# Self-attention rounds of a four-layer Perceiver kernel: statistics one tile further ahead, another order on every engine

## The reference

```python
x = x + L1_attn(layernorm(x))   # 8 heads of 32, keys and values from a latent of 64
x = x + L2_attn(layernorm(x))   # 16 query heads of 8, 4 key heads; RMS norm, rotation
x = x + L3_attn(layernorm(x))   # 16 heads of 8, hyperbolic distance

# L1: probs = softmax(q k^T / sqrt(32));  out = (probs v) Wo
# L2: q, k = rotate(rms_norm(q)), rotate(rms_norm(k))
#     s = 50 tanh(q k^T / sqrt(8) / 50), causal;  out = (softmax(s) v) Wo
# L3: diff = max(|q|^2 + |k|^2 - 2 q k^T, 0)
#     denom = max((1 - |q|^2)(1 - |k|^2), 1e-6)
#     out = (softmax(-arccosh(1 + 2 diff / denom)) v) Wo
```

## Time and profile before

| | |
|---|---|
| median of 3 runs | 7111.27 us (7109.43 to 7120.28) |
| the profiled execution's own time | 7113.01 us |
| its span, first to last instruction | 7110.8 us |
| mean granted TensorE clock | 0.902 of 2.4 GHz |
| busy: TensorE, weight loads, VectorE, ScalarE, GpSimd | 82%, 65%, 55%, 40%, 26% |

### The profile page before, as it was taken

The page is one execution under the profiler, slowest core; times in us unless marked ns, Lnnn a source line. Parts: engine busy times, 40 slices in busy tenths (PEclk is TensorE's granted clock), DMA queues, the critical chain, the costliest instruction groups (busy, mean ns, idle before and its releaser), DMA issues.

```text
span 7110.8 us, 164674 instructions
## 1 busy us (share of the span) xinstructions
PE 5839.7 (82%) x53890; PEld 4596.3 (65%) x53890; DVE 3933.1 (55%) x12136; ACT 2811.1 (40%) x6643; POOL 1823.1 (26%) x2870
## 2 busy tenths in 40 slices
PE   6888888788779998878888998676679987778888
PEld 4666666777447776656665777664457766666666
DVE  5766665444336664544444665664446659964443
ACT  2444443111234442245544555223435542235555
POOL 3444443000013333300000343660014434320000
PEclk9999999999769998999998999678779997779999
DMA  3000000000000000000000110000001100000000
GB/s 126 16 16 16 16 16 8 0 0 0 0 15 30 30 24 0 0 0 0 0 0 9 34 33 24 0 0 0 0 15 33 33 18 0 0 0 0 0 0 12
DMA packets 43764, 93.43 MB, mean 13 GB/s; under 512 B 7696, under 2 KB 28560, under 8 KB 42640
## 3 DMA queue, kind: packets, MB, share of 16 engines
q1 hardware_dynamic: 43664, 92.09, 4.1%
HBM read 88.92 MB, written 3.15 MB: 13 GB/s over the span
## 4 chain that ended last, share of the span: by engine, by line
issue 47%; PE 35%; DVE 8%; POOL 6%; ACT 2%; SPq 1%; POOLq 0%; DVEq 0%; DMA 0%; ACTq 0%
PE psum_banks L548 5%; PE psum_banks L553 4%; PE psum_banks L613 3%; PE psum_banks L657 3%; PE psum_banks L664 2%; PE psum_banks L617 2%; PE psum_banks L1598 2%; PE psum_banks L1574 2%; PE psum_banks L1633 2%; POOL scratch L957 2%; PE psum_banks L1072 1%; DVE scratch L919 1%; POOL scratch L1495 1%; POOL scratch L924 1%; PE psum_banks L1586 1%
## 5 line engine op out<-in xcount | busy, mean ns | idle before, releaser
L2271 PE MATMUL psum_banks<-w_L_ffn_up,x_normed_T 128*128 128x352 f32 (+3 forms) x2112 | 871.8, 535 | 90.4 <-DVE x_normed_T L2413 56.9
L263 POOL TENSOR_TENSOR ln_vareps<-ln_meanvar,ln_eps 128x1 f32<-128x1 f32 x165 | 44.6, 270 | 2794.5 <-DVE ln_meanvar L258 2794.5
L780 DVE TENSOR_REDUCE scratch<-psum_banks 128x2 f32<-128x514 f32 x768 | 531.0, 691 | 411.1 <-PE psum_banks L548 407.0
L699 ACT ACTIVATE scratch<-psum_banks 128x512 f32<-128x512 f32 x768 | 458.5, 597 | 491.1 <-PE psum_banks L558 485.8
L553 PE MATMUL psum_banks<-scratch 32*128 32x128 f32 x6144 | 639.3, 310 | 8.2 <-ACT scratch L699 6.1
L2309 ACT ACTIVATE scratch<-psum_banks 128x176 f32<-128x176 f32 (+3 forms) x1120 | 398.6, 371 | 619.8 <-PE psum_banks L2271 526.9
L548 PE MATMUL psum_banks<-scratch 32*128 32x257 f32 x3072 | 575.5, 441 | 50.2 <-DVE scratch L781 50.1
L2257 PE MATMUL psum_banks<-w_L_ffn_down,scratch 128*128 128x128 f32 x4096 | 563.7, 285 | 10.4 <-ACT scratch L2300 10.4
L2249 PEld LDWEIGHTS psum_banks<-consts,scratch 128*128 128x128 f32 x2144 | 280.5, 154 | 444.7 <-issue 295.5
L2271 PEld LDWEIGHTS psum_banks<-w_L_ffn_up,x_normed_T 128*128 128x128 f32 x2112 | 407.0, 218 | 221.7 <-issue 106.5
L2453 DVE SCALAR_TENSOR_TENSOR scratch<-scratch,psum_banks 128x176 f32<-128x176 f32 (+2 forms) x704 | 257.6, 373 | 524.7 <-ACT scratch L2309 492.2
(11 more groups left out here) (426 smaller groups left out, 14236.7 us busy)
## 6 DMA issues: line engine op xcount, KB each, us to landing
scratch<-in_ctx SPq DMA_DIRECT2D x99, 514.0 KB, 3.5
scratch<-in_ctx_rows SPq DMA_DIRECT2D x130, 128.0 KB, 2.1
w_L_ffn_up<-in_L_ffn_up SPq DMA_DIRECT2D x1, 2992.0 KB, 10.5
w_L_ffn_down<-in_L_ffn_down SPq DMA_DIRECT2D x1, 2112.0 KB, 12.1
w_L_ffn_up<-in_L_ffn_up SPq DMA_DIRECT2D x1, 2080.0 KB, 7.9
x_tokens<-in_x SPq DMA_DIRECT2D x1, 2048.0 KB, 7.7
scratch<-last_values SPq DMA_DIRECT2D x128, 8.0 KB
out<-x_tokens SPq DMA_DIRECT2D x1, 2048.0 KB, 6.3
```

The source lines that it names most:

```text
L699: act.activation(pT[:, b % 2, 2 * h:2 * h + 2].rearrange("p t c q -> p t (c q)"), W, ACT.Exp).then_inc(exp_ready.sem, 1)
L780: dve.tensor_reduce(parts[:, r.t.odd, 2 * h:2 * h + 2, 0, b], S, X_AXIS, ALU.max, negate=True)
L2271: pe.matmul(U[g % 3][:, 0:fw * halves], k.xnT[:, :], up[:, c0:c0 + fw * halves], start=True, stop=True).then_inc(sg["up_written"].sem, 1)
```

## The change

- All three stages: statistics move from tile r+2 to tile r+3 (`third`), to the end of VectorE's round ahead of residual, and `normal` to the end of GpSimd's round. `normalised` stays with tile r+2 and goes to the front of VectorE's round (in the third stage behind two steps). The plan begins one round earlier.
- First stage: on VectorE heads(r-1) goes ahead of operands(r+1).
- Second stage: VectorE's order becomes normalised, rotate, mask, squares, heads, operands, statistics, residual. GpSimd's power is now for tile r+2 and stands behind its two spreads. TensorE's turn(r) goes behind project and middle. ScalarE's take_x goes ahead of Tanh and Exp, take_qkv ahead of take_middle.
- Third stage: TensorE's scores(r+1) go ahead of heads(r-1). 1 - sum is now made on TensorE: the matrix has -1 in place of 1, and a product of a row of ones with itself adds 1 (two products more). take_middle goes, and VectorE reads the result from PSUM. GpSimd does its four spreads in one run.

The diff, cut to its core (`...` for what is left out):

```diff
@@ chain, plan
-    plan = Plan(1, TILES - 3, TILES + 1, 2, -2)
+    plan = Plan(1, TILES - 3, TILES + 1, 2, -3)
@@ GpSimd, one(r)
             if kind == "L1":
-                if r.after:
-                    normal(r.t + 2)
                 if r.coming:
...
                     values(t, s["kv"][:, 256:512])
             if kind == "L2":
-                if r.coming:
-                    pool.wait_ge(ms_ready.sem, ms_ready.at(t, 1))
-                    pool.wait_ge(rotated.sem, rotated.at(r.t, 1))
-                    pool.tensor_tensor(s["r"][:, :], s["ms"][:, :], k.minus_half[:, 0:20], ALU.pow).then_inc(rms_ready.sem, 1)
-                if r.after:
-                    normal(r.t + 2)
...
+                if r.after:
+                    pool.wait_ge(ms_ready.sem, ms_ready.at(r.t + 2, 1))
+                    pool.wait_ge(rotated.sem, rotated.at(t, 1))
+                    pool.tensor_tensor(s["r"][:, :], s["ms"][:, :], k.minus_half[:, 0:20], ALU.pow).then_inc(rms_ready.sem, 1)
...
+            if r.third:
+                normal(r.t + 3)
@@ TensorE
         def middle(t):
-            pe.wait_ge(mid_read.sem, mid_read.at(t + -1, 1))
+            if kind == "L3":
+                pe.wait_ge(operands.sem, operands.at(t + -1, 1))
+            else:
+                pe.wait_ge(mid_read.sem, mid_read.at(t + -1, 1))
...
-                    mm = pe.matmul(MID[:, n * P:(n + 1) * P], k.c("same_head"), s["sq"][:, n * P:(n + 1) * P], start=True,
-                                   stop=True, skip_group_check=True)
+                    cols = slice(n * P, (n + 1) * P)
+                    pe.matmul(MID[:, cols], k.c("minus_same_head"), s["sq"][:, cols], start=True, stop=False,
+                              skip_group_check=True)
+                    mm = pe.matmul(MID[:, cols], one, one, start=False, stop=True, skip_group_check=True)
...
-            if kind != "L3" and r.own:
+            if kind == "L1" and r.own:
                 turn(r.t)
...
+            if kind == "L2" and r.own:
+                turn(r.t)
+            if kind == "L3" and r.coming:
+                scores(r.t + 1)
             if r.turned:
                 heads(r.t + -1)
-            if r.coming:
+            if kind != "L3" and r.coming:
                 scores(r.t + 1)
@@ ScalarE, second stage
-            elif r.own:
+            if kind == "L2" and r.after:
+                take_x(r.t + 2)
+            if kind == "L2" and r.own:
                 act.wait_ge(scores_written.sem, scores_written.at(r.t, 1))
                 act.activation(s["D"], D[:, :], ACT.Tanh, scale=float(1.0 / (CAP * np.sqrt(8.0)))).then_inc(scores_read.sem, 1)
...
@@ VectorE, stats and one_l2(r)
-            if r.after:
-                link(dve.bn_stats(k.stat[:, :], k.X[:, (r.t + 2).index(), :]), r, "stats")
+            if r.third:
+                link(dve.bn_stats(k.stat[:, :], k.X[:, (r.t + 3).index(), :]), r, "stats")
...
-            stats(r)
+            normalised(r)
+            if r.coming:
+                rotate(r)
             if r.own:
...
-            if r.coming:
-                rotate(r)
-            normalised(r)
-            heads(r)
...
                 dve.tensor_scalar(s["ms"], s["ms"], 0.125, 1e-5, ALU.mult, ALU.add).then_inc(ms_ready.sem, 1)
+            heads(r)
...
+            stats(r)
             residual(r)
@@ VectorE, one_l3(r)
-            stats(r)
...
+            normalised(r)
...
-                dve.wait_ge(mid_read.sem, mid_read.at(t, 1))
-                rows_by_head(dve, s["rest"], s["ab"][:, 0:P], k.c("lane_eighth"))
+                dve.wait_ge(mid_written.sem, mid_written.at(t, 1))
+                rows_by_head(dve, s["rest"], MID[:, 0:P], k.c("lane_eighth"))
+                rows_by_head(dve, s["kbd"][:, 2, :], MID[:, P:2 * P], k.c("quad")).then_inc(operands.sem, 1)
...
-            normalised(r)
-            if r.coming:
-                rows_by_head(dve, s["kbd"][:, 2, :], s["ab"][:, P:2 * P], k.c("quad")).then_inc(operands.sem, 1)
             heads(r)
...
+            stats(r)
             residual(r)
```

More of the change, by code:

```diff
@@ L346, in __init__ @@
         r = plan.loop if t.i is not None else t.o
-        self.after, self.coming, self.own, self.turned, self.ended, self.left = (
-            0 <= r + d < TILES for d in (2, 1, 0, -1, -2, -3))
+        self.third, self.after, self.coming, self.own, self.turned, self.ended, self.left = (
+            0 <= r + d < TILES for d in (3, 2, 1, 0, -1, -2, -3))
 class PerTile:
@@ L1191, in one @@
             if r.after:
-                take_x(r.t + 2)
                 if kind == "L1":
-                    take_qkv(r.t + 2)
-            if kind == "L2":
-                if r.coming:
-                    take_middle(r.t + 1)
-                if r.after:
-                    take_qkv(r.t + 2)
+                    take_x(r.t + 2)
+                take_qkv(r.t + 2)
+            if kind == "L2" and r.coming:
+                take_middle(r.t + 1)
             if r.turned:
@@ L1305, in one_l2 @@
                                   ).then_inc(probs_ready.sem, 1)
-            if r.coming:
-                rotate(r)
-            normalised(r)
-            heads(r)
-            if r.coming:
-                t = r.t + 1
-                dve.wait_ge(mid_read.sem, mid_read.at(t, 1))
-                dve.wait_ge(scores_written.sem, scores_written.at(r.t, 1))
-                rows_by_head(dve, s["qbd"][:, 0, :], s["qkT"][:, 0:P], k.c("lane")).then_inc(operands.sem, 1)
             if r.after:
@@ L1321, in one_l2 @@
                 dve.tensor_scalar(s["ms"], s["ms"], 0.125, 1e-5, ALU.mult, ALU.add).then_inc(ms_ready.sem, 1)
+            heads(r)
+            if r.coming:
+                t = r.t + 1
+                dve.wait_ge(mid_read.sem, mid_read.at(t, 1))
+                dve.wait_ge(scores_written.sem, scores_written.at(r.t, 1))
+                rows_by_head(dve, s["qbd"][:, 0, :], s["qkT"][:, 0:P], k.c("lane")).then_inc(operands.sem, 1)
+            stats(r)
             residual(r)
```

30 lines of the change are left out of this document (11 added, 19 removed).

## The result

The changed kernel takes 7040.72 us (median of 4, 7029.06 to 7041.88), the kernel before 7110.35 beside it on the same chip (median of 4): a ratio of 0.9894, 95% interval 0.9878 to 0.991, 1.1% faster. 7043 was forecast. The profiled execution took 7040.86 us and spans 7039.0.

The account below looks back on a forecast made before the run. Bounds: first stage TensorE waiting for xn, second a ring through GpSimd's power, third VectorE with stretched instructions. -54 + 12 - 26 = -68 against 7113.0 gives 7045, by the median 7043 us; range 6996 to 7086.

Parts of the forecast that it names:

- -54 forecast: First stage: xn follows residual at once, turn_x waits for values alone; rounds 10.89 to 9.1 us, -54 us.
- The 8.97 us of TensorE work: First stage: TensorE's work in a row from turn_x to turn_x without the wait, the low end of a round.
- +12 forecast: Second stage: rounds of 11.7 us, 0.4 more than before, +12 us (ends -40 and +68).
- The chain: Second stage: values, turn_x, take_x, Tanh, Exp, mask, squares, heads, scores, output follow through every engine; 9.9 us at 2.4 GHz.
- 9.9 at 2.4 GHz: Second stage: the round in us with TensorE at the full clock throughout, the low end, worth -40 us.
- -26 forecast: Third stage: less VectorE stretching and waiting, rounds 15.35 to 14.3 us, -26 us (ends -45 and +10).
- the wait for output should be gone: Third stage: output starts 12.7 us into the round, so VectorE's 0.6 us a round of idle time ahead of residual goes.
- take_qkv behind take_heads: Third stage, ScalarE: take_qkv ends some 0.6 us after 12.7, squares due at 13.3; +10 us if 1.4 us late mostly.
- Rival 1: Second stage gains too, as the clock rises: 9.9 to 10.3 us a round, -32 us, 6999 in all; chance 0.14.
- Rival 2: Third stage gains nothing: scores first delay heads, take_qkv and squares, three full stretches stay; 7077 us; chance 0.18.
- Rival 3: First stage keeps a wait: GpSimd's L924 holds the L919 pair, scores wait; 10.0 us a round, 7071; chance 0.08.
- Rival 4: Slower: TensorE stays at 1.2 GHz in second and third stages, +68 and +38 us, 7163 in all; chance 0.04.

Follow-up runs that it names:

- e4: The changed kernel, but in the second stage ScalarE does Tanh and Exp ahead of take_x again: 6995.23 us (0.9845 of the kernel before).
- e8: The changed kernel with six extra unread TensorE products between turn and heads in the second stage: 7002.27 us (0.9852 of the kernel before).
- e11: The changed kernel, but the third stage's sum reads bank D from PSUM, with the maximum with 0 in the same VectorE instruction: 7037.56 us (0.9894).
- e9: The changed kernel, but in the third stage ScalarE copies the sums to SBUF again and VectorE's two products read that copy: 7071.19 us (0.9952).
- e5: The changed kernel, but in the third stage TensorE does heads(r-1) ahead of scores(r+1) again: 7039.28 us (0.9906 of the kernel before).

## Why the prediction was right, point by point

**First stage: -54 forecast, -58 measured.** xn at once, turn_x with no wait, GpSimd's pair and VectorE's stretched pair both beside heads: all as worked out. The clock of the loop is 0.98, as expected. The mis-sized part is the round, 9.1 against 8.94: 8.8 us in all but two rounds, which take 10.5. The 8.97 us of TensorE work, used as the floor, counts values up to the end of its last pass, but turn_x begins before that: at 2836.24 in the round above, 0.16 us ahead of the end of values.

**Second stage: +12 forecast, +15 in the whole change and +13 alone.** The chain holds term by term in the round above: values 1.85 us (1.8 forecast), turn_x and take_x 0.6 (0.7), Tanh and Exp 1.33 (1.4), squares 1.73 (1.7), scores 1.92 (2.05 at 1.2 GHz). The mask was taken at 0.7 and is 0.96. The clock shows most in the scores: before, they took 1.13 us in 16 of 27 rounds and about 2.05 in the others; now they take 1.8 us or more in 24 of 27. How much of the loss is this and how much the chain, no run tells. "ScalarE's take_x ahead of Tanh" was named as the reason, and e4 shows it. That transposes do not count as busy for the clock gate in the same way, by the Trainium skill (TensorE: Matmul & The Clock Gate, Part 4: PE-mode transpose), would by the prediction's estimate have made 11.9 us and more. 11.71 came, with the granted clock at 0.71 before and after, so here nothing of it was seen, and no run tells turn's part apart.

What the text missed is a size: it spoke of "9.9 at 2.4 GHz" as an end, and the way there was open. Heads and scores at 2.4 GHz in every round are worth 38 us (e8), and the clock could be had for six unused products.

**Third stage: -26 forecast, -29 in the whole change, -22 alone.** How near the number comes is in part luck: of the -29 some 5 us lie ahead of the stage's first residual, and 14.49 us a round is the best of six traces of this code. In the five others the stage saves 16 to 18 us from first to last residual. That the stretch would leave L1341's successor, meet L1331's, stay on xn and on the first product, and spare those that read PSUM, is what the groups show. The stretches left are 0.87 + 0.57 + 0.72 = 2.16 us a round, 2.0 forecast. The Trainium skill (SBUF — State Buffer, SBUF: two separate sides) gives as the reason that VectorE and GpSimd share a pair of ports: VectorE's two-port forms use it, and so do its instructions with two SBUF inputs, against a GpSimd instruction that reads SBUF. The trace agrees in which instructions are hit (1541 ns against 676 for the same product), and e11 and e9 show it in both directions; held in full, 2.4 us, they are not always.

One step failed: "the wait for output should be gone" because scores stand first. The wait is gone, and it was credited with 0.6 of the 1.0 us. But e5 has it back and loses nothing, since the stretching shrinks as the waiting grows. What the gain cannot do without is the reading from PSUM: e9, which has scores first and no wait, is no better than before. Whether that reading alone would bring the gain in the old order, no run shows. I added two terms that are one: while GpSimd spreads, VectorE either waits or is held. "take_qkv behind take_heads" is a real wait, which the sum put at nothing: 1.7 us in all in the profiled execution, 6.5 to 8.0 in the five other traces (most of what they are slower by), none with heads first (e5).

**The rivals.** Rival 1 (second stage gains) fell in this kernel but its condition was right: with the clock up, e8 has 10.2 us a round, inside its 9.9 to 10.3. Rival 2 (third gains nothing) had the delay through take_qkv, which is there, but at 0.06 us a round in this trace and 0.24 to 0.30 in the others; the stage gains all the same. Rival 3's stretched pair exists, 2.02 us, and costs nothing. Rival 4 needed the second stage's clock below 0.55; it is 0.71.

## What to carry to other kernels

Before an engine's in-order list puts a new step ahead of an old one, ask which of the two has its inputs first: one copy moved ahead of Tanh cost some 40 us here, where the whole change brought 70. And look at more than one trace before a difference of half a microsecond a round is put down to an edit: the changed kernel's own trace is here the exception of six. Where TensorE idles a few us in each round and comes back at 1.2 GHz, a handful of unread products in the pause may pay; try it early, it is one line. And do not add a removed wait and a removed stretch on the same engine without asking whether they are the same time: take one away alone and see whether the other grows.

## What was not expected of the hardware

- Six unread products a round raised the granted clock of the second stage's loop from 0.73 to 0.99 and took 38 us off the kernel, 11.71 to 10.21 us a round.
- The clock can alternate from round to round in one loop: heads 2.07 and 1.16 us in neighbouring rounds of e4, rounds of 11.5 and 9.0.
- GpSimd's power on 128x20 takes 3.54 us, yet does not hold VectorE up: L920, which reads SBUF twice, ran beside it in 0.68 us (4569.14 in the second stage's timeline, and 0.68 in all 27 rounds), where beside a spread the same product takes 1.54 in the third stage.
- A stretch that is taken from one instruction goes in part to the next that reads SBUF twice: L1342 takes 884 ns in e11, 676 in the changed kernel's trace and 724 to 768 in the five others of its code.
- In e9 the second of the three products takes 1.52 us in 16 of 26 rounds and 0.68 in the other ten, with nothing between.
